# A transformer block on eight images: softmax sums divided out of the chunk outputs instead of the probabilities, and a front in two halves

## What is computed

```python
x = x + attention(layernorm_over_channels(x))     # 8 heads of 64 channels, softmax over 1024 keys, f32
t = tokens(x)
t = t + ffn(layernorm_over_channels(t))           # decodes 4 nibbles of a token, three small layers, adds to few channels
```

## Time and profile before

| | |
|---|---|
| median of three runs | 2576.1 us |
| the profiled execution | 2574.47 us, span 2572.7 us |
| mean granted TensorE clock | 0.989 |
| TensorE busy | 2463.3 us, 96% |
| VectorE busy | 1940.7 us, 75% |
| ScalarE busy | 1731.3 us, 67% |
| GpSimd busy | 910.2 us, 35% |
| DMA | 215.14 MB, mean 84 GB/s |

### The profile page before, as it was taken

The page is one execution under the profiler, slowest core; times in us unless marked ns, Lnnn a source line. Parts: engine busy times, 40 slices in busy tenths (PEclk is TensorE's granted clock), DMA queues, the critical chain, the costliest instruction groups (busy, mean ns, idle before and its releaser), DMA issues.

```text
span 2572.7 us, 37174 instructions
## 1 busy us (share of the span) xinstructions
PE 2463.3 (96%) x13216; PEld 2019.5 (78%) x13216; DVE 1940.7 (75%) x3599; ACT 1731.3 (67%) x3083; POOL 910.2 (35%) x812
## 2 busy tenths in 40 slices
PE   7999999999999999999999999999999999999986
PEld 5788778888788887887878877788787887778874
DVE  4777777787777877778777787777867778677756
ACT  4777557775677746777477783777737776477744
POOL 1344414444144432444314434244422444134431
PEclk8999999999999999999999999999999999999997
DMA  7223303341133312224122331232403223123210
GB/s 266 72 67 106 111 19 93 87 132 66 50 83 77 121 66 66 70 74 136 50 71 74 78 133 40 78 82 63 156 17 89 76 70 143 34 83 78 67 70 33
DMA packets 80550, 215.14 MB, mean 84 GB/s; under 512 B 10384, under 2 KB 10608, under 8 KB 74608
## 3 DMA queue, kind: packets, MB, share of 16 engines
q1 hardware_dynamic: 80368, 212.77, 27.6%
HBM read 102.63 MB, written 25.17 MB: 50 GB/s over the span
## 4 chain that ended last, share of the span: by engine, by line
PE 78%; DVE 11%; ACT 7%; issue 2%; POOL 1%; DMA 1%; SPq 0%; ACTq 0%; DVEq 0%
PE pT L468 16%; PE pJ L434 10%; PE pO L483 9%; PE pO L484 9%; PE pS L455 8%; PE pS L456 8%; PE po L619 7%; PE pv L592 3%; DVE PL L885 2%; PE pv L434 2%; ACT PR L699 2%; ACT PH L733 1%; PE pa L630 1%; POOL PR L386 1%; PE pa L535 1%
## 5 line engine op out<-in xcount | busy, mean ns | idle before, releaser
L386 POOL TENSOR_SCALAR PR<-PR,rinv 128x1024 f32<-128x1024 f32 x512 | 577.2, 1127 | 1226.9 <-DVE rinv L857 1226.9
L733 ACT ACTIVATE PH<-pT 128x512 fp32r<-128x512 f32 x1024 | 557.3, 597 | 361.6 <-PE pT L468 348.8
L885 DVE TENSOR_TENSOR PL<-pT,PH 128x512 fp32r<-128x512 f32 x1024 | 657.4, 684 | 178.9 <-ACT PH L733 176.7
L853 DVE TENSOR_REDUCE nmax<-pS 128x1 f32<-128x1024 f32 x512 | 623.8, 1218 | 148.4 <-PE pS L456 147.5
L699 ACT ACTIVATE PR<-pS,nmax 128x1024 f32<-128x1024 f32 x512 | 575.2, 1123 | 5.5 <-DVE nmax L853 2.3
L468 PEld LDWEIGHTS pT<-ident,PR 128*128 128x128 f32 x4096 | 465.9, 141 | 128.9 <-POOL PR L386 48.6
L468 PE MATMUL pT<-ident,PR 128*128 128x128 f32 x4096 | 544.7, 275 | 22.4 <-DVE PL L885 15.6
L483 PE MATMUL pO<-PH,VS 128*128 128x512 f32 x1024 | 418.1, 408 | 6.3 <-DVE PL L885 6.3
L455 PE MATMUL pS<-KHL,QS 128*128 128x512 f32 x1024 | 412.7, 403 | 3.1 <-DMA KHL<-KHL 2.3
L456 PE MATMUL pS<-KHL,QS 128*128 128x512 f32 x1024 | 404.7, 395 | 0.0
L484 PE MATMUL pO<-PL,VS 128*128 128x512 f32 x1024 | 404.3, 395 | 0.0
(11 more groups left out here) (171 smaller groups left out, 3054.3 us busy)
## 6 DMA issues: line engine op xcount, KB each, us to landing
KHL<-HL SPq DMA_DIRECT2D x192, 256.0 KB, 3.4
X<-in_x SPq DMA_DIRECT2D x64, 512.0 KB, 6.5
WQ<-wqk_split SPq DMA_DIRECT2D x62, 512.0 KB, 4.2
QS<-HL SPq DMA_DIRECT2D x192, 128.0 KB, 3.1
WO<-wo_split SPq DMA_DIRECT2D x16, 1024.0 KB, 7.0
out<-X SPq DMA_DIRECT2D x16, 1024.0 KB, 5.0
KHL<-wv_split SPq DMA_DIRECT2D x14, 1024.0 KB, 9.2
KHL<-KHL SPq DMA_DIRECT2D x16, 512.0 KB, 4.2
```

The costliest lines, as they stand in the source:

```text
L386: pool.tensor_scalar(PR[g % 2][:, :], PR[g % 2][:, :], M["rinv"][:, g:g + 1], 1.0, ALU.mult, ALU.mult)\
L733: act.activation(PH[ck % 2][:, 4 * half:4 * half + 4, (g % 4) * P:(g % 4 + 1) * P], pT[half][:, :].rearrange("p (k n) -> p k n", k=4), ACT ...
L853: dve.tensor_reduce(nmax[:, g:g + 1], pS[g % 2][:, :], AX.X, ALU.max, negate=True).then_inc(S["a_max"], 1)
L885: dve.tensor_tensor(PL[ck % 2][:, ks, qs], pT[half][:, :].rearrange("p (k n) -> p k n", k=4), f32(PH[ck % 2][:, ks, qs]), ALU.subtract).th ...
```

## The change

1. The division leaves the probabilities. `turn` waits for the exponential, and the transposed, unnormalised exponentials go into the values. The reciprocals are taken four columns at a time, once per chunk. SyncE writes them to DRAM as a row of 512 floats (`reciprocals_out`) and reads that row into 64 partitions of a new tile RB (`reciprocals_in`). GpSimd multiplies the chunk's output in OT by RB and adds v's bias (`scale_output`), two instructions of 64x512; `a_o` now counts these, and a new `a_osum` VectorE's sum. On GpSimd the scale of chunk ck stands at step 4(ck + 2), that of chunk 15 behind H0 (E68). In SyncE's order the reciprocals of a chunk stand behind each copy of HL, and the last ones around the loads of WV and X1.
2. Image 0's layer norm runs in two halves of four tokens (N10 and N20), with a semaphore of its own, and the splitting of Wv (W0) goes from ScalarE and VectorE to GpSimd.
3. The orders of all engines at the seams are written anew. The steps 4 to 63 now stand in them too, in unchanged order; of these runs only the first and last line is shown.

```diff
@@ buffers @@
+        rs_s = nc.dram_tensor("rinv_rows", (2 * HEADS, 512), F32, kind="Internal").ap()
+                                   (82 * KB, "RB", [P, 512], F32), (76 * KB, "XN", [P, ST, SEL], F32), (76 * KB + 3584, "G", [P, ST, 2, 5], F32),
-            "small": [(b_qk[:, :], bqk), (b_v[D:P, :], bv), (bo_all[:, :], bo_rep), (ramp[:, :], ramp_d),
+            "small": [(b_qk[:, :], bqk), (b_v[0:D, :], bv), (b_v[D:P, :], bv), (bo_all[:, :], bo_rep), (ramp[:, :], ramp_d),
@@ orders written out @@
 START = {
-    "tensor": """T0 T1 T2 T3 T4 T5 T6 T7 B0 B1 B2 V0 B3 B4 B5 V1 V2 B6 V3 V4 B7 V5 V6 V7 Q0 Q1 Q2 Q3 P0 P1 A0 A1 A2 A3""",
-    "scalar": """W0 T0 T1 T2 T3 T4 T5 T6 T7 N0 B0 W1 B1 B2 W2 B3 B4 B5 V0 V1 V2 B6 V3 W5 W3 B7 V4 V5 V6 V7 Q0 Q1 Q2 Q3
+    "tensor": """T0 T1 T2 T3 T4 T5 T6 T7 B0 B1 B2 V0 V1 B3 B4 V2 B5 B6 V3 V4 V5 B7 V6 V7 Q0 Q1 Q2 Q3 P0 P1 A0 A1 A2 A3""",
+    "scalar": """T0 T1 T2 T3 T4 T5 T6 N10 T7 W2 B0 B1 B2 N20 V0 W3 V1 B3 B4 W1 B5 B6 V2 V3 V4 W5 B7 V5 V6 V7 Q0 Q1 Q2 Q3
         A-1 A0 A1 A2 A3""",
-    "vector": """T0 T1 T2 T3 T4 T5 T6 T7 N0 W0 B0 B1 B2 V0 B3 W2 V1 V2 B4 B5 W1 B6 V3 W4 V4 W3 B7 V5 V6 V7 Q0 Q1 Q2 W5
+    "vector": """T0 T1 T2 T3 N10 T4 T5 T6 T7 B0 B1 N20 W2 W4 B2 V0 V1 B3 B4 W1 V2 W3 V3 B5 B6 V4 V5 B7 V6 V7 Q0 Q1 W5 Q2
         A-1 D3 A0 A1 A2 A3""",
-    "gpsimd": """N0 A0 A1 A2 A3""",
+    "gpsimd": """W0 N10 N20""",
 }
 EDGE = {
-    "tensor": """T0 T1 E65 E66 E67 T2 T3 T4 T5 T6 T7 O0 O1 O2 O3 O4 O5 O6 O7 B0 B1 U0 U1 B2 U2 B3 U3 B4 U4 U5 V0 U6 U7 V1
-        B5 V2 V3 V4 B6 B7 V5 V6 F0 F1 V7 L0 F2 F3 Q0 L1 L10 L2 L11 L20 L3 Q1 L12 L21 Q2 L22 L13 P0 L23 P1 Y0 Q3
-        A0 R0 R1 R2 R3 A1 R4 R5 A2 R6 R7 A3""",
-    "scalar": """H0 H1 H2 T0 T1 T2 T3 E67 T4 T5 H3 T6 T7 N0 B0 B1 U0 U1 B2 U2 U3 U4 U5 U6 U7 V0 B3 S0 B4 B5 V1 V2 V3 V4
-        B6 B7 V5 F0 V6 F1 V7 L0 F2 F3 L1 L10 L2 L11 L20 Q0 Q1 L12 L21 L3 Q2 L13 L22 L23 A-1 Q3 A0 R0 R1 R2 R3 A1
-        R4 R5 A2 R6 R7 A3""",
-    "vector": """H0 T0 T1 T2 T3 T4 E67 T5 H1 H2 O0 T6 T7 O1 O2 N0 O3 H3 O4 O5 O6 O7 B0 B1 U0 U1 U2 U3 U4 U5 B2 U6 U7 V0
-        S0 B3 S5 V1 S1 V2 B4 S2 B5 V3 V4 B6 B7 S3 V5 V6 L0 V7 L1 L10 L2 L11 Q0 Q1 L12 L3 Q2 L13 A-1 S4 D3 A0 A1
-        A2 A3""",
-    "gpsimd": """H0 N0 S0 F0 A0 A1 A2 A3""",
+    "tensor": """E4 E5 E6 E7 E8 E9 E10 E11 E12 E13 E14 E15 E16 E17 E18 E19 E20 E21 E22 E23 E24 E25 E26 E27 E28 E29 E30
...
+        E57 E58 E59 E60 E61 E62 E63 T0 E65 E66 E67 T1 T2 T3 T4 T5 T6 T7 O0 O1 O2 O3 O4 O5 O6 O7 U0 U1 B0 B1 U2
+        U3 B2 B3 U4 U5 B4 V0 U6 U7 V1 V2 B5 B6 V3 B7 V4 V5 V6 F0 F1 V7 L0 F2 F3 Q0 L1 L10 L2 L11 L20 Q1 L12 L21
+        L3 Q2 L22 L13 P0 P1 L23 Y0 Q3 A0 R0 R1 A1 R2 R3 R4 R5 A2 R6 R7 A3""",
+    "scalar": """E4 E5 E6 E7 E8 E9 E10 E11 E12 E13 E14 E15 E16 E17 E18 E19 E20 E21 E22 E23 E24 E25 E26 E27 E28 E29 E30
...
+        E57 E58 E59 E60 E61 E62 E63 H0 H1 T0 T1 H2 E67 T2 T3 T4 T5 T6 T7 N0 H3 U0 U1 B0 B1 U2 U3 U4 B2 B3 U5 U6
+        U7 B4 V0 S0 V1 V2 V3 B5 B6 B7 V4 V5 V6 F0 F1 L0 F2 F3 V7 L1 L10 L2 L11 L20 Q0 Q1 L12 L21 L3 Q2 L13 L22
+        L23 A-1 Q3 A0 R0 R1 A1 R2 R3 R4 R5 A2 R6 R7 A3""",
+    "vector": """E4 E5 E6 E7 E8 E9 E10 E11 E12 E13 E14 E15 E16 E17 E18 E19 E20 E21 E22 E23 E24 E25 E26 E27 E28 E29 E30
...
+        E57 E58 E59 E60 E61 E62 E63 T0 H0 T1 H1 E67 H2 T2 T3 T4 T5 T6 T7 N0 O0 O1 O2 O3 O4 H3 O5 O6 O7 U0 B0 B1
+        U1 U2 U3 U4 U5 B2 B3 U6 U7 V0 S0 S5 V1 S1 V2 B4 S2 V3 B5 B6 B7 V4 S3 V5 V6 L0 V7 L1 L10 L2 L11 Q0 Q1 L12
+        L3 Q2 L13 A-1 S4 D3 A0 A1 A2 A3""",
+    "gpsimd": """E7 E8 E11 E12 E15 E16 E19 E20 E23 E24 E27 E28 E31 E32 E35 E36 E39 E40 E43 E44 E47 E48 E51 E52 E56 E60
+        E64 H0 E68 N0 S0 F0""",
 }
 LAST = {
-    "tensor": """E65 E66 E67 O0 O1 O2 O3 O4 O5 O6 U0 U1 U2 U3 O7 U4 U5 U6 U7 F0 L0 F1 L10 L1 F2 F3 L20 L2 L11 L3 L12 L21
-        Y10 L22 L13 R0 R1 R2 L23 R3 Y20 R4 R5 R6 R7""",
-    "scalar": """H0 H1 E67 H2 H3 U0 U1 U2 U3 S10 U4 U5 U6 U7 F0 S20 F1 L0 L10 L1 F2 F3 L2 L20 L11 L3 L12 L21 L22 L13 R0
-        R1 R2 L23 R3 R4 R5 R6 R7""",
-    "vector": """E67 H0 H1 O0 O1 O2 H2 H3 O3 O4 O5 O6 U0 U1 U2 U3 S10 O7 S15 S11 U4 S12 U5 S13 U6 U7 S20 S25 S21 S22 L0
-        S23 L10 L1 L2 L11 L3 L12 S14 L13 S24""",
-    "gpsimd": """H0 S10 F0 F2""",
+    "tensor": """E4 E5 E6 E7 E8 E9 E10 E11 E12 E13 E14 E15 E16 E17 E18 E19 E20 E21 E22 E23 E24 E25 E26 E27 E28 E29 E30
...
+        E57 E58 E59 E60 E61 E62 E63 E65 E66 E67 O0 O1 O2 O3 O4 O5 O6 U0 U1 U2 U3 O7 U4 U5 U6 U7 F0 L0 F1 L10 L1
+        F2 L20 F3 L2 L11 L3 L12 L21 Y10 L22 L13 R0 R1 R2 L23 R3 Y20 R4 R5 R6 R7""",
+    "scalar": """E4 E5 E6 E7 E8 E9 E10 E11 E12 E13 E14 E15 E16 E17 E18 E19 E20 E21 E22 E23 E24 E25 E26 E27 E28 E29 E30
...
+        E57 E58 E59 E60 E61 E62 E63 E67 H0 H1 H2 H3 U0 U1 U2 U3 S10 U4 U5 U6 U7 S20 F0 F1 L0 L10 L1 F2 F3 L2 L11
+        L20 L3 L12 L21 L22 L13 R0 R1 R2 L23 R3 R4 R5 R6 R7""",
+    "vector": """E4 E5 E6 E7 E8 E9 E10 E11 E12 E13 E14 E15 E16 E17 E18 E19 E20 E21 E22 E23 E24 E25 E26 E27 E28 E29 E30
...
+        E57 E58 E59 E60 E61 E62 E63 E67 H0 H1 H2 O0 O1 O2 O3 O4 O5 H3 O6 U0 U1 U2 U3 S10 O7 S15 S11 U4 U5 S12 U6
+        U7 S13 S20 S25 S21 S22 L0 S23 L10 L1 L2 L11 L3 L12 S14 L13 S24""",
+    "gpsimd": """E7 E8 E11 E12 E15 E16 E19 E20 E23 E24 E27 E28 E31 E32 E35 E36 E39 E40 E43 E44 E47 E48 E51 E52 E56 E60
+        E64 H0 E68 S10 F0 F2""",
 }
 
 
...
-        order += [("A", i, g) for g in range(4, 64)] + work(EDGE if i + 1 < N_IMG else LAST, i)
+        order += [("A", i, g) for g in range(4, 4)] + work(EDGE if i + 1 < N_IMG else LAST, i)
@@ sync_program @@
+    def reciprocals_out(i, ck):
+        wait("a_recip", i, ck + 1)
+        sp.dma_start(dram["rs"][ck].rearrange("(j p) -> p j", p=P), M["rinv"][:, 4 * ck:4 * ck + 4],
+                     allow_slow_non_contiguous=True).then_inc(S["a_row"], 16)
+
+    def reciprocals_in(i, ck):
+        wait("a_row", i, 16 * (ck + 1))
+        if ck >= 2:
+            wait("a_omul", i, ck - 1)
+        elif i > 0:
+            wait("a_omul", i - 1, 2 * HEADS)
+        half = slice(ck % 2 * D, (ck % 2 + 1) * D)
+        sp.dma_start(M["RB"][half, :], dram["rs"][ck].unsqueeze(0).to_broadcast([D, 512])).then_inc(S[f"a_rows{ck % 2}"], 16)
 
...
         if i > 0:
             store(i - 1)
+        reciprocals_out(i, 0)
         for h in range(2, HEADS):
             wait("a_scores", i, ST * (h - 1))
             for n in range(NCH):
+                k = NCH * (h - 2) + n
                 cs = slice(n * 512, (n + 1) * 512)
                 wait("a_proj_lo", i, NCH * (h - 2) + n + 1)
                 for half in range(2):
                     ps = slice(half * D, (half + 1) * D)
                     sp.dma_start(f32(QS[h % 2][ps, cs]), f32(HL[0:D, half, :])).then_inc(S["a_qk"], 16)
                     sp.dma_start(f32(KHL[h % 2][ps, :, cs]), f32(HL[D:P, :, :])).then_inc(S["a_qk"], 16)
+                reciprocals_in(i, k)
+                reciprocals_out(i, k + 1)
             if h + 2 < HEADS:
                 weights(h + 2, f"a_w{h % 2}")
         wait("a_proj", i, NCH * (HEADS - 2))
...
         if i + 1 < N_IMG:
             for t in range(CT):
                 sp.dma_start(M["X"][:, t, :], dram["x"][i + 1, :, t, :]).then_inc(S["f_x"], 16)
-            for k in range(2):
-                wait("a_scores", i, ST * (HEADS - 1 + k))
-                sp.dma_start(f32(WV[k].rearrange("p k n -> p (k n)")), dram["wv"][:, k, :]).then_inc(S["f_wv"], 16)
+        reciprocals_in(i, 12)
+        if i + 1 < N_IMG:
+            wait("a_scores", i, ST * (HEADS - 1))
+            sp.dma_start(f32(WV[0].rearrange("p k n -> p (k n)")), dram["wv"][:, 0, :]).then_inc(S["f_wv"], 16)
+        reciprocals_out(i, 13)
+        reciprocals_in(i, 13)
+        reciprocals_out(i, 14)
+        reciprocals_in(i, 14)
+        if i + 1 < N_IMG:
+            wait("a_scores", i, ST * HEADS)
+            sp.dma_start(f32(WV[1].rearrange("p k n -> p (k n)")), dram["wv"][:, 1, :]).then_inc(S["f_wv"], 16)
+        reciprocals_out(i, 15)
         wait("a_pv", i, 2 * HEADS)
         for t in range(CT):
             sp.dma_start(M["X1"][:, t, :], dram["x"][i, :, t, :]).then_inc(S[f"b_x{t}"], 16)
+        reciprocals_in(i, 15)
         if i + 1 < N_IMG:
             wait("f_back", i + 1, 4)
             for h in range(2):
@@ gpsimd_program @@
+    def scale_output(img, ck):
+        h, n = divmod(ck, 2)
+        part = slice(n * D, (n + 1) * D)
+        o = M["OT"][part, :, h * P:(h + 1) * P]
+        wait("a_osum", img, ck + 1)
+        wait("a_proj_lo", img, min(ck + 1, PER["a_proj_lo"]))
+        if ck == 2 * HEADS - 1:
+            wait("b_bias", img, 2 * CT)
+        wait(f"a_rows{n}", img, 16 * (h + 1))
+        pool.tensor_tensor(o, o, M["RB"][part, :].rearrange("d (j m) -> d j m", j=CT), ALU.mult).then_inc(S["a_omul"], 1)
+        wait("a_omul", img, ck + 1)
+        pool.tensor_scalar(o, o, M["b_v"][part, h:h + 1], None, ALU.add).then_inc(S["a_o"], 1)
+        wait("a_o", img, ck + 1)
+
     for kind, img, g in order:
-        if kind == "A" and 0 <= g < STEPS:
```

(47 more changed lines are left out.)

68 lines of the change are left out of this document (36 added, 32 removed).

## The result

The changed kernel takes 2685.3 us (median of 4 runs, 2674.7 to 2690.0) against 2576.1: a ratio of 1.042 [1.040, 1.043], where the prediction had 2556 and a range to 2572. It is 109 us slower.

What follows compares the result with a forecast made beforehand. TensorE was taken as the bound, busy 2463.3 of 2572.7 us. The terms 0 - 8 - 8.5 - 3.5 + 5 - 2 - 5.5 + 2.5 = -20 took 2576.1 to 2556 us, range 2536 to 2572.

Steps and rivals of the forecast that it cites:

- Steps beside projections: Attention steps running beside the next head's projections: TensorE has no gap, rows arrive about 3 us early; 0 us.
- rival C: Head's first scores: rows land late, GpSimd's scale delays the next HL; slower, 1 us over gives 2604 us; chance 0.13.
- the other moves: Remaining reorderings within the seam of two images (U before B): 1 us each way per seam, taken as -2 us.
- the opening: Image 0's opening steps: the divisions' 1.1 us leaves the chain of exponential, reciprocal, division and transposes; -2 us.
- (a): Seam, 7 times: the reciprocal leaves VectorE, `results` starts 1.1 to 1.4 us earlier; -1.2 us each, -8.5 us.
- steps without projection: Each image's last 14 steps, 8 times: PL starts earlier without the reciprocal, waits for GpSimd's divisions go; -8 us.
- rival B: Only the front gains; ScalarE sets the pace at seams and OT steps; 2573 to 2578, say 2574 us; chance 0.13.
- (b): Seam, 7 times: T1 moves behind E67, giving ScalarE a token's time; -0.5 us each, -3.5 us.
- E67: Step in the engines' order at the seam; moving T1 behind it was to give -0.5 us each, -3.5 us.
- (c): Seam: chunk 15's scale stands behind GpSimd's eight bias adds, so O6 waits for OL; +0.7 us each, +5 us.
- The front, -5.5: Image 0's front: V0 2.8 us earlier, copy of K -0.7, opening steps -2; -5.5 us in all.
- The last image, +2.5: Last image's tail: O6 waits for O5's add and OL, +2.1; ScalarE's H0 behind E67's OB, +0.4; +2.5 us.

Runs made afterwards that it cites:

- the front alone: Kernel of before with only image 0's new front (W0 on GpSimd, statistics in halves, new opening order); division, steps and seams of before: 2571.4 us, ratio 0.998.
- the division undone: Changed kernel with the division back on the probabilities and no row DMAs, new front and orders kept: 2629.9 us; with N0 behind O2 as well, 2581.3 us.
- no rows: Changed kernel without its 256 row DMAs; GpSimd multiplies by a constant tile, so outputs are not divided by the sums: 2609.7 us, ratio 1.013.
- the writes alone: Changed kernel with only the 128 DMAs out of 512 single floats; none read back, GpSimd multiplies by a constant tile: 2677.7 us, ratio 1.041.
- N0 moved: Whole changed kernel, writes still in 4-byte pieces, with VectorE's N0 behind O2 instead of ahead of O0: 2717.3 us, ratio 1.055.

## Why the prediction was wrong

By difference of kernels the 109 us are: the front -7 (the front alone); the other orders without N0 +10 (the division undone with N0 behind O2, less the front alone); N0 +51 (the division undone, with N0 ahead and behind); the division -20 (no rows, less the division undone); the writes +75 (the changed kernel less no rows). The terms hold in this order only, since the last two causes share a place.

*Steps beside projections: "The cost is 0."* **This step failed.** It gave the 16 writes of an image the time of their issue on SP's queue, 1.4 us per chunk with the read, and put at nothing what the transfer itself does to the ones behind it; "it is issued a whole chunk ahead of its reader" stood for that. The bounds it named, nothing and rival C's stalls, were the right ones. A write of 512 single floats takes 9.0 us to landing, and the writes alone, with nobody waiting for one inside an image, cost 68 us. In the whole change writes and reads cost 75: over the kernel without rows the steps of images 0 to 6 are 44 us longer and the seams 29. Two things had been left out. First, the copies of HL, the weights and X1 share the queue with the write, and land late. Second, "a whole chunk ahead" holds for chunks 0 to 11; for chunks 12 to 15 SP writes and reads back one after the other, and each write's 9 us or more stand ahead of X1's issue.

The place of rival C was right (PE ahead of a head's first scores, 3.9 us at 790.61), and it was given 0.13. Most of the writes' 75 us lie in its stretch, though not by the way it gave alone: it wanted the rows late and POOL's scale ahead of HL, and in the kernel with the writes alone PE waits 34.6 us at the same place with POOL waiting for no row. The 3.4 us for the read were right where the queue is quiet (3.8 in the median) and not in images 2, 5 and 6.

The Trainium skill's rule on a strided last dimension (DMA: Bandwidth & Descriptors, Rules for kernel authors) holds in the profile's packets: 65,536 of the new ones are the 512 floats of 128 writes. The estimate of 5.4 us, from the packet price in the same page's Measured section, was too small: the runs show 9.0 us, and most of that is not packets (last section). "The sum would be the same by it" was the error: neither figure was set against what stands behind the write.

*The seam: "the other moves ... have no row that prices them: 1 us each way".* **This step failed too**, and it need not have. The row of f_ev at 300.78 us (1.07 us) was used against the front's plan and not against the seam's, where the same change puts the whole chain beside POOL's additions and ahead of O0. The chain is 5.7 us long there, and PE loses 5.1 us by standing and 1.5 by the clock at a seam, 46 us at seven; the kernels say 51, the second largest term.

**The other terms, and luck.** The kernel with 16-byte pieces and N0 behind O2 shows them without the two failures. Cut at the rows of PE as above, its profiled execution is shorter (-) or longer (+) than that of before by:

```
us                                              forecast   measured
front, to the first transposes                    -3.5       -6.4
image 0's first four steps (the opening)          -2         -0.8
first four steps of images 1 to 7 (a)             -8.5       -9.6
steps beside projections (4 to 49)                 0         -5.0
steps without projection (50 to 63, images 0-6)   -8         +2.3
the seven seams (b, c and the other moves)        -0.5       +1.4
last image behind step 49                         +2.5       +0.5
sum                                              -20        -17.6
```

The sum is that of the profiled spans, 2555.2 less 2572.7; by the medians the kernel is 21 us faster.

So that the sum came out near -20 is in part luck. (a) was right in size, and PE's 8.2 us of waits for X from `results` are gone at the seams. *The -8 of the steps without projection* was wrong: they gave 1.2 us, and in image 2, where PE waits 1.9 us for a late copy of HL at 869.8, 3.5 were lost again. The waits for POOL went (5.6 us), but those for PL rose from 15.6 to 21.4, which is what rival B says of the place. *Beside projections*, where 20.00 of 20 us were busy and nothing was expected, 5.0 us came: from an image's fourth chunk on a chunk takes 13.69 to 13.75 us there and took 13.72 to 13.83. A stretch that looks full can still hold 0.1 us in 14, and no run tells what set them. In the kernel of before and in that with the front alone an image's first four steps take 15.0 us in some images and 16.0 or 16.1 in others, so the third line is good to some 2 us.

*(b) T1 behind E67, -3.5.* Wrong sign: PE's waits for a token and those of the values for PL are 10.3 and 9.2 us in that kernel, against 6.4 and 6.3 before; putting the order back gave nothing either. The 10 us of the other orders were measured with the old division, and are not split further.

*(c) chunk 15's scale, +5.* 0: with X1 in time the additions start at 282.78, and OL is not waited for at a seam. The term took 291.05 from the trace of before, while the front and T1's move bring the seam forward.

*The front, -5.5.* It is made of 2.8 for V0, 0.7 for the copy of K and 2 for the opening, which hangs on the division. The front alone, with the old division, gave 6.7: more than its 3.5. Its rows in the changed kernel:

```profile
11.48 1.89 POOL L443 CAST KHL<-rawv 128x2048 fp32r<-128x2048 f32 x1 [11.04 <-DMA rawv<-in_wv]
13.45 4.52 POOL L445 TENSOR_TENSOR KHL<-rawv,KHL 128x2048 fp32r<-128x2048 f32 x1
14.46 3.54 DVE L958 TENSOR_SCALAR f_ev<-f_mv 128x4 f32<-128x4 f32 x1
19.54 3.02 POOL L467 TENSOR_SCALAR XT<-XT,f_r,f_nb 128x512 f32<-128x512 f32 x4 [1.57 <-DVE f_nb L980]
22.98 1.89 PE L655 MATMUL pv<-KHL,XH 128*128 128x512 f32 x4
61.18 0.50 PE L516 MATMUL pS<-KHL,QS 128*128 128x512 f32 x1 [1.24 <-DMA KHL<-KHL]
```

f_ev is 3.54 us long and ends with POOL's subtraction, as foreseen (at 18.0 and not 18.9, as POOL's two took 6.4 us and not 7.5); V0 is at 22.98 (23.8 foreseen, 26.64 before), the first scores at 61.18 wait 1.24 us for the copy of K (2.28 before: -1.0 for -0.7). These two make the first scores 4.9 us earlier; the first transposes behind them are 6.2 us earlier, and the last 1.3 us had no term. The Trainium skill's rule on the pair (SBUF — State Buffer, SBUF: two separate sides) agrees with these rows: f_ev ends at 18.00 us and POOL's subtraction at 17.97.

*The last image, +2.5.* O6's wait came as foreseen (1.9 us for OL), and about as much fell away elsewhere.

So the sum of -20 is near the time of a kernel that the change is not: it needs writes in pieces of 16 bytes and N0 behind O2, and that kernel took 2556.8 us.

## What to carry to other kernels

Before a DMA is called hidden, ask two things: what it does to the transfers behind it on the queue while it is under way, and who stands behind a wait for it in the issuing engine. A 2 KB row written as 512 single floats cost 68 us in 128 writes that nobody waited for, and 75 with the waits and the reads; written as 128 pieces, with the same waits, it cost nothing. Let each partition's floats leave as one piece and let the reader permute, which cost nothing here. And once a row shows one engine holding the small operations of another, look through the whole new order for every place where such a chain is set ahead of something that TensorE waits for.

## What the runs showed of the hardware

What a write in 4-byte pieces costs is not in its own packets. Queue 1's share times the span gives the engines' time: 247 us more with the writes alone than without rows (35.6% of 2678.0 less 27.1% of 2607.2), 1.93 us of all 16 engines for each of 128 writes. But by the records of the single packets those of 4 bytes take 9 ns in the median, as those of 8 and of 16 bytes do in the other kernels, and only 40 of the 247 us are theirs. The rest is in the packets of other transfers, which take longer: those of 4 KB 296 ns in the mean and not 178, those of 8 KB 627 and not 392. From 16-byte to 8-byte pieces the engines' time grows by 0.25 us a write (33.0% of 2559.0 less 31.8% of 2555.2).

The write also lands long after its packets. DMA's occupancy from 272 to 282 us of the changed kernel (40 slices of 0.25 us), around chunk 14's write, issued at 272.48 and landed at 281.76:

```profile
DMA  0000899403675000000000000000000000000000
DMA packets 608, 0.13 MB, mean 13 GB/s; under 512 B 544, under 2 KB 544, under 8 KB 608
```

The 64 packets over 512 B are chunk 13's read, in the first block and at the start of the second; the rest of the second is the write, from 274.5 to 275.3 us. From then on no packet is shown, and SP goes on 6.5 us later. With 16-byte pieces the same write took 2.4 us, 0.6 of them behind its last packet; with 8-byte pieces 4.2 us, 2.0 behind it. So that time grows as the pieces get smaller, at the same 2 KB. No run tells what passes in it.

Also open is why the reads take 7 to 9 us in the median of images 2 and 5 and some of 6, and 3.6 in the others, with SP's issues in the same order. These are the images whose steps are long in all four kernels with 4-byte pieces and reads (232, 223 and 218 us in the changed kernel, 240, 234 and 226 with N0 moved, where a quiet image has 212). In the kernel with the writes alone it is images 1, 4 and 6 (240, 229 and 222 us), and in 1 and 4 the copies of HL are slow. So which images are slow, and by how much, makes the times of all kernels with 4-byte pieces uncertain as a measure of a single edit, and 23 of the 32 us that moving N0 seemed to cost lie in these steps.
